# An attention stage with folded projections, and a latent loop regrouped by heads and written out

## What is computed

```python
h = h + attn(layernorm(h))                # 8 heads of width 128, biases on q, k and v, softmax, @ Wo
h = h + latent(layernorm(h))

# latent: G=8 groups of H=16 heads, D=128, L=100 latents
xn = l2norm(x) * gamma
q = xn @ Wq + bq ; k, v = split(xn @ Wkv + bkv)
w = (softmax(silu(k @ aw1 + b) @ aw2 + b, -1) / s + softmax(.., -2) / L) / 2
kc, vc = einsum('bsd,bsl->bld', k, w), einsum('bsd,bsl->bld', v, w)   # per group
att = softmax(q . kc / sqrt(D))           # b, g, h, s, l
z = att . vc                              # 16384 wide per token
h1 = silu(l2norm(z) * g1 @ W1 + b1)       # 256 wide
out = silu(l2norm(h1) * g2 @ W2 + b2)
```

## Time and profile before

| | us |
|---|---|
| median of 3 runs | 3341.05 |
| the runs | 3330.03 to 3342.83 |
| the profiled execution | 3334.86 |
| its span, first to last instruction | 3332.0 |
| attention, 704.9 to 1315.4 | 610.5 |
| latent prologue, 1318.4 to 1383.3 | 64.9 |
| latent loops with both tails, 1383.3 to 3332.0 | 1948.7 |

### The profile page before, as it was taken

How to read it: one execution, slowest core, us unless ns; L and a number is a source line. 1 busy time by engine, 2 the same in 40 slices (tenths; PEclk the granted TensorE clock), 3 DMA queues, 4 the chain that set the end, 5 groups by cost and what they waited for, 6 DMA issues and landing times.

```text
span 3332.0 us, 57433 instructions
## 1 busy us (share of the span) xinstructions
PE 3032.7 (91%) x18996; PEld 2666.2 (80%) x19032; DVE 2402.0 (72%) x4368; ACT 1797.5 (54%) x3135; POOL 1772.1 (53%) x1524
## 2 busy tenths in 40 slices
PE   3488885979999998799999999999799999999997
PEld 3266664868888887599999999998699999999986
DVE  2499896356676676577777777776677777777774
ACT  0398893446566564255555555554455555555544
POOL 5698883010100001366666666675467666666663
PEclk9899996989999999799999999999899999999998
DMA  1111100000000001000000000000000000000000
GB/s 43 40 29 24 25 20 26 0 35 0 0 0 0 0 0 46 19 30 29 28 28 28 28 28 19 28 28 29 10 29 28 28 28 28 28 28 28 28 27 7
DMA packets 36972, 75.92 MB, mean 23 GB/s; under 512 B 9644, under 2 KB 13876, under 8 KB 36120
## 3 DMA queue, kind: packets, MB, share of 16 engines
q1 hardware_dynamic: 35352, 71.68, 6.8%
q0 software_dynamic: 1536, 3.15, 0.4%
HBM read 65.36 MB, written 1.05 MB: 20 GB/s over the span
## 4 chain that ended last, share of the span: by engine, by line
PE 49%; issue 5%; POOL 3%; DVE 1%; ACT 0%; POOLq 0%; DVEq 0%; ACTq 0%
PE lat_ps_h L1837 20%; PE lat_ps_z L1851 10%; PE lat_ps_s L1763 7%; PE lat_ps_t L1790 6%; PE lat_ps_z L1781 3%; POOL lat_zz L1570 2%; PE lat_ps_z L1773 2%; PE lat_ps_z L1861 1%; POOL latm_wq L1549 0%; POOL latm_wq L1543 0%; POOL latm_att L1562 0%; POOL latm_vcg L1554 0%; PE lat_ps_s L1879 0%; DVE latm_norm L1669 0%; DVE latm_h L1675 0%
## 5 line engine op out<-in xcount | busy, mean ns | idle before, releaser
L1837 PE MATMUL lat_ps_h<-latm_share,latm_attT 100*128 100x256 f32 x6144 | 885.9, 286 | 0.0
L1837 PEld LDWEIGHTS lat_ps_h<-latm_share,latm_attT 100*128 100x128 f32 x6144 | 818.7, 189 | 24.0 <-DVE latm_attT L1626 11.1
L1562 POOL TENSOR_TENSOR latm_att<-latm_sc,latm_tot 128x400 f32<-128x400 f32 x516 | 440.6, 854 | 618.7 <-DVE latm_tot L1621 592.2
L1570 POOL TENSOR_TENSOR lat_zz<-lat_zz,lat_zsq 128x512 f32<-128x512 f32 x514 | 659.7, 1283 | 0.3
L1698 ACT ACTIVATE latm_sc<-latm_sc 128x400 f32<-128x400 f32 x516 | 278.4, 539 | 430.8 <-DVE latm_sc L1612 430.8
L1851 PE MATMUL lat_ps_z<-latm_attT,latm_vg 100*128 100x512 f32 x1536 | 486.8, 425 | 0.0
L1619 DVE TENSOR_REDUCE latm_tot<-latm_sc 128x4 f32<-128x400 f32 x516 | 290.9, 564 | 156.9 <-ACT latm_sc L1698 156.9
L1626 DVE TENSOR_TENSOR latm_attT<-lat_ps_t,latm_attT 100x512 fp32r<-100x512 f32 x514 | 349.8, 681 | 61.3 <-ACT latm_attT L1714 61.3
L1714 ACT CAST latm_attT<-lat_ps_t 100x512 fp32r<-100x512 f32 x514 | 300.3, 584 | 147.8 <-PE lat_ps_t L1790 122.8
L1763 PE MATMUL lat_ps_s<-latm_wk,lat_xr 128*128 128x400 f32 x1548 | 370.1, 348 | 3.0 <-issue 3.0
L1719 ACT ACTIVATE lat_zsq<-lat_ps_z 128x512 f32<-128x512 f32 x512 | 306.9, 599 | 59.1 <-PE lat_ps_z L1851 22.2
(11 more groups left out here) (339 smaller groups left out, 4816.0 us busy)
## 6 DMA issues: line engine op xcount, KB each, us to landing
lat_w_in<-in_w_quads SPq DMA_DIRECT2D x65, 512.0 KB, 3.6
lat_wq_in<-in_wq_quads SPq DMA_DIRECT2D x65, 256.0 KB, 2.6
ret_qk_head<-ret_qk_parts SPq DMA_DIRECT2D x256, 32.0 KB, 2.0
moe_w<-in_W SPq DMA_DIRECT2D x2, 1024.0 KB
mha_wqk<-in_Wqk SPq DMA_DIRECT2D x1, 1152.0 KB, 5.4
ret_shared<-in_xpos_q SPq DMA_DIRECT2D x1, 1024.0 KB, 5.6
ret_shared<-in_xpos_k SPq DMA_DIRECT2D x1, 1024.0 KB, 4.9
latw_wkv<-in_Wkv SPq DMA_DIRECT2D x1, 1024.0 KB
```

The source lines that it names most:

```text
L1562: nc.gpsimd.tensor_tensor(att[:, u].rearrange("p (j l) -> p j l", j=QH), sc[:, u].rearrange("p (j l) -> p j l", j=QH), tot[:, u].unsqueeze ...
L1570: nc.gpsimd.tensor_tensor(zz[:, t], zz[:, t], zsq[:, u], ALU.add).then_inc(s["zz_added"], 1)
L1837: mm = e.matmul(ps_h[:, t, :], attT[:, t % 2, a_part, j * P:(j + 1) * P], share[:, u, w_part, j * FF2:(j + 1) * FF2], start=False, stop=Fa ...
```

## The change

Attention. Wq and Wk of each head are multiplied once into one matrix, Wv and Wo likewise, with the biases (`fold`, `fold_bias`; the means of Wq and Wk are first taken out on VectorE and added on GpSimd). q is no longer made: scores are xr (the normed input plus one, `lift`) times keys made with the folded matrix. v with Wo in it lands directly in the output's space, so that `output` goes, and all heads of a sequence add up in PSUM. That needs probabilities that are divided before they are turned: GpSimd multiplies the 128x1024 tile by the inverse sum. The 128 steps are written out, with scores two steps ahead and `gather` seven behind.

Latent loop. The step is now one head with four tiles: `add` uses share as stationary operand and attT (512 tokens) as moving one, 6 products of 512 columns in place of 12 of 256; the result is kept transposed (`ps_h` is [feature, token]), so that the tail needs no transposes. Scores, with their softmax, run LEAD = 6 steps ahead of the addition, with 8 slots of `att`. wk and share go into the free bank of ps_s, after the scores. All 512 steps (both sequences) are written out as one row; the tail of the first sequence is put into steps of the second (`MIDDLE`), that of the second starts in its last steps (`ENDING`). Square roots and silu are made from Newton steps on VectorE and tanh on ScalarE.

```diff
+        @block.gpsimd                       # attention
+            e.wait_ge(weights_in, 112)
+            nc.gpsimd.tensor_copy(bv_wide[:], bv[:].unsqueeze(2).to_broadcast([P, H, P])).then_inc(s["bv_widened"], 1)
+            e.wait_ge(s["qk_mean"], START + 2)
+            nc.gpsimd.tensor_tensor(wqT[:], wqT[:], wide(mean[:, 0]), ALU.add).then_inc(s["q_centred"], 1)
+            nc.gpsimd.tensor_tensor(wkT[:], wkT[:], wide(mean[:, 1]), ALU.add).then_inc(s["k_centred"], 1)
...
+            for step in range(K):
+                e.wait_ge(s["inv_ready"], START + step + 1)
+                nc.gpsimd.tensor_scalar(probs[:, step % 4], probs[:, step % 4], inv[:, step % TB:step % TB + 1], None, ALU.mult
+                                        ).then_inc(s["normed"], 1)
+                if step >= 1 and makes_values(step - 1):
+                    low_values(*makes_values(step - 1))
...
+            fold()                          # attention, tensor
             norm.tensor(e)
+            fold_bias()
...
+            for step in range(K + 14):
+                if LAG <= step < K + LAG:
+                    gather(step)
+                if step >= 1 and makes_keys(step - 1):
+                    n, c = makes_keys(step - 1)
+                    e.wait_ge(s["keys_ready"], START + 2 * n + c + 1)
...
+                if 2 <= step <= K + 1:
+                    turn(step - 2)
+                if step + 2 < K:
+                    score(step + 2)
+                if makes_keys(step):
+                    make_keys(n, c, psT[:, 0, :])
+                if makes_values(step):
+                    make_values(n, half, psT[:, 0, :])
...
+            norm.vector(e, means)           # attention, vector: means stands ahead of sum_squares
...
+                def add(n):                 # latent, tensor
...
+                    for a_part, w_parts in ((0, (0, 1)), (1, (0,))):
+                        if a_part == 1:
+                            e.wait_ge(s["attT_ready"], START + n + 1)
+                        for f in range(2):
+                            for w_part in w_parts:
+                                cols = slice(j * FF2 + f * P, j * FF2 + (f + 1) * P)
+                                mm = e.matmul(ps_h[:, f, half, :], share[:, q % 2, w_part, cols], attT[:, n % 2, a_part],
...
-                for a_part, w_part in ((0, 0), (0, 1), (1, 0)):
-                    for j in range(QH):
-                        mm = e.matmul(ps_h[:, t, :], attT[:, t % 2, a_part, j * P:(j + 1) * P],
-                                      share[:, u, w_part, j * FF2:(j + 1) * FF2],
...
+                def turn(n):
+                    half, j = n % TB // 4, n % 4
+                    if j == 0:
+                        e.wait_ge(s["weighted"], START + n + 4)
+                    e.wait_ge(s["attT_ready"], START + n)
+                    for i in range(4):
+                        mm = e.transpose(ps_t[0:L, i * P:(i + 1) * P], att[:, (n - j + i) % SLOTS, j * L:(j + 1) * L], ident[:])
...
+                for n in range(-LEAD, END):
+                    k = n + LEAD
+                    if n - 1 >= -LEAD:
+                        free_spare(n - 1)
+                    if k < K:
+                        score(k)
+                    if makes_wk(n):
+                        e.wait_ge(s["shifted"], START + k)
+                        make_wk(quad(k) + 1, spare_bank(n))
+                    if makes_share(n):
+                        e.wait_ge(s["shifted"], START + k)
+                        make_share(quad(n) + 1, n % TB - 4, spare_bank(n))
...
+                    if 0 <= n < K:
+                        add(n)
+                    if 0 <= n + 1 < K:
+                        turn(n + 1)
+                    if 0 <= n < K:
+                        reduce_heads(n)
...
+                def inverse_root(which, step, floor, done):   # latent, vector
+                    x, y = sums[:, which], inv[:, which]
...
+                        c.then(e.tensor_tensor(newton[:], y, y, ALU.mult))
+                        c.then(e.tensor_tensor(newton[:], newton[:], x, ALU.mult))
+                        c.then(e.tensor_scalar(newton[:], newton[:], -0.5, 1.5, ALU.mult, ALU.add))
+                        c.then(e.tensor_tensor(y, y, newton[:], ALU.mult))
...
+            MIDDLE = {"norm": 0, "root": 0, "spread": 4, "wide": 8, "scale": 8, "tanh": 9, "gate": 10, "square": 10,
+                      "power": 16, "power_root": 16, "result": 24, "pre": 24, "out_tanh": 24, "out": 25}
```

More of the change, by code:

```diff
@@ L1008, in _ @@
[L1008 to L1018 removed]
+            wide = lambda a: a.unsqueeze(2).to_broadcast([P, H, D])
+            e.wait_ge(weights_in, 112)
@@ L1059, in _ @@
[L1059 to L1087 removed]
+            e.wait_ge(s["wqk_ready"], START + 1)
@@ L1131, in _ @@
+            for step in range(K + 14):
+                if step < K:
+                    exponentials(step)
+                for b, c in closes(step):
+                    keep_out(b, c)
+                if 2 <= step <= K + 1:
+                    high(step - 2)
+                if step >= 1 and makes_values(step - 1):
+                    high_values(*makes_values(step - 1))
+                if makes_keys(step):
+                    high_keys(*makes_keys(step), psT[:, 0, :])
         @block.vector
@@ new lines, in low, with add_out @@
+            def low(k):
+                i = k % TB
+                for half in range(2):
+                    high, rest = (probsT[:, part, 4 * half:4 * half + 4, i * P:(i + 1) * P] for part in range(2))
+                    e.wait_ge(s[f"high_ready{half}"], START + k + 1)
+                    e.tensor_tensor(rest, psT[:, half, :].rearrange("p (j s) -> p j s", j=4), high.bitcast(F32),
+                                    ALU.subtract).then_inc(s[f"low_ready{half}"], 1)
+            def add_out(b, c):
+                t = b * TB + 4 * c
+                e.wait_ge(s["out_turned"], START + 2 * b + c + 1)
+                e.tensor_tensor(h[:, t:t + 4], psT[:, 0, :].rearrange("p (t d) -> p t d", t=4), h[:, t:t + 4], ALU.add).then_inc(s["out_added"], 1)
@@ new lines, in _ @@
+            for c in range(2):
+                low_keys(0, c, psS[:, 0, c, :])
+            e.wait_ge(s["bvo_ready"], START + 1)
+            for half in range(2):
+                full_values(0, half, psO[:, half, :])
+            maxima(0)
+            for step in range(K + 14):
+                if step + 1 < K:
+                    maxima(step + 1)
+                if 2 <= step <= K + 1:
+                    low(step - 2)
+                if step < K:
+                    invert(step)
+                if makes_keys(step):
+                    low_keys(*makes_keys(step), psT[:, 0, :])
+                if makes_values(step):
+                    full_values(*makes_values(step), psT[:, 0, :])
+                for b, c in adds_out(step):
+                    add_out(b, c)
@@ new lines, in latent, with when, due, rooting @@
+            STEPS = 4
+            END = K + 8
+            def when(b, c, stage):
+                if b == 0:
+                    return NS + TB + 4 * TB * c + MIDDLE[stage]
+                return ENDING[c][stage]
+            def due(n, stage):
+                return [(i, b, c) for i, (b, c) in enumerate(units) if when(b, c, stage) == n]
+            def rooting(n, stage):
+                done = []
+                for i, (b, c) in enumerate(units):
+                    per = 1 if b == 0 else 2 if (c, stage) == (0, "root") else STEPS
+                    first = per * (n - when(b, c, stage))
+                    done += [(i, step) for step in range(first, first + per) if 0 <= first < STEPS]
+                return done
@@ new lines, in root_of_power, with scale_h @@
+                def root_of_power(i, step):
+                    if step == 0:
+                        e.wait_ge(s["power_kept"], START + i + 1)
+                        e.wait_ge(s["pre_ready"], START + i)
+                    inverse_root(1, step, 4e-24 / FF2, "power_inverted")
+                def scale_h(i, half, bank):
+                    e.wait_ge(s["wide_ready"], START + i + 1)
+                    e.wait_ge(s["h_kept"], START + 2 * i + 2)
+                    for f in range(2):
+                        c.then(e.tensor_tensor(hT[:, half, f], bank, hT[:, half, f], ALU.mult))
+                    e.sem_inc(s["h_scaled"], 1)
+                    for f in range(2):
+                        last = e.tensor_scalar(hT[:, half, f], hT[:, half, f], b1[:, f:f + 1], None, ALU.add)
+                    last.then_inc(s["h_biased"], 1)
```

1173 lines of the change are left out of this document (593 added, 580 removed).

## The result

The changed kernel takes 3195.83 us in the median (3195.40 to 3197.89) against 3335.54 for the kernel before: a ratio of 0.958, with an interval of 0.956 to 0.961. Forecast were 3248 and a range of 3170 to 3310. The gain is 140 us where 93 were expected. The profiled execution has a span of 3194.1 us.

A forecast was written before the change was run, and what follows sets the result against it. TensorE was taken as the bound, 99% busy in both loops and 97% in the attention. Gains of 38 + 34 + 11 - 3 + 13 = 93 us gave 3248 us by the median; range to give 3170 to 3310.

The forecast's parts named there:

- rival A: Latent loop: TensorE's edges and gaps go, steps 3.02, a quad 27.3 or so; 70 us more gained, 3178; chance 0.20.
- Attention, steady part: Attention units: 33.3 us each in place of 36.28, as q's and the output's products go; gain 49 us.
- rival B: Attention: GpSimd's tensor_scalar takes 4.1, units come to about 36, the gain of 49 shrinks to 6; 3291; chance 0.13.
- Attention, start: Before the first attention unit: means wait for all weight transfers, folding runs on slow TensorE; 11 us later, bounds 4 and 17.
- Latent step: Plain latent steps: time goes by columns, so regrouping to 512 columns gives 0; steps stay 3.10, bounds +31 and -41 us.
- The quad: Four latent steps with wk and two shares inserted: extra falls from 3.67 to 3.47; latent steps gain 34, bounds 100 and -40.
- t = 2: Latent step ahead of wk, VectorE's late step of 3.37: 0.27 goes, as the mean of wq moves behind the low part.
- First tail: First sequence's tail, moved into the second loop: 48.4 us go, 37 come in, 1.3 a root step; gain 11, bounds 19 and 65.
- End: Second sequence's tail at the kernel's end: 44.3 us become about 31; gain 13, bounds 22 and 4.
- C: Latent loop: VectorE blocked at every root and inserted steps at their upper bound; 3320; chance 0.08.
- D: Latent loop: `turn` with j == 0 waits for weighted probabilities, forecast ready 0.9 us early; if late, 256 us more, 3504; chance 0.05.
- E: Attention: the folding removes no TensorE work, so the change doesn't do what it says; given nothing.

The follow-up runs named there:

- pool_longer: Changed kernel with an additional GpSimd product of 128x416 ahead of each attention weighting; 3280.2 us on another chip, 57 us more from the attention on.
- before_bank: Kernel before, with wk and the two shares put into the free bank of the scores (ps_s) in place of ps_z; 3304.6 us.
- before_bank_mean: before_bank with the mean of wq moved on VectorE from behind the shift to behind the low part of the additions; 3354.9 us.
- before_unrolled: Kernel before with only its latent loop written out, eight copies in place of the hardware loop; 3324.3 us.
- before_bank_unrolled: before_bank with its latent loop written out; 3314.5 us on another chip, 19 us less than before_bank from the attention on.

## Why the prediction was right, and where it was wrong

The direction was forecast, and the attention with its mechanism; the size of the whole was not: 93 us of gain were forecast and 140 came. 3195.8 lies outside the forecast's own 3215 to 3285, and it is inside the range given because that was widened for rival A, whose mechanism did not come: that part is luck. One term was badly off, the inserted work of a quad.

- Attention, steady part: right to the tenth, in part because two terms were off in opposite ways. Timeline of TensorE, first half of v for the second and the sixteenth unit; and the group of GpSimd's product:

```profile
766.87 1.05 PE L986 MATMUL mha_psT<-mha_wvo,xT 128*128 128x128 f32 x8
...
1232.35 1.05 PE L986 MATMUL mha_psT<-mha_wvo,xT 128*128 128x128 f32 x8
```
```profile
L946 POOL TENSOR_SCALAR mha_probs<-mha_probs,mha_inv x128: 2841/2848/2858, 747.4 to 1266.7; 128x1024 f32<-128x1024 f32 x128
```

  (1232.35 - 766.87) / 14 = 33.25, forecast 33.3. By distances from scores to scores, eight plain steps are 3.65 each (forecast 3.71, 0.5 less a unit), the keys with their wait 2.2 (forecast 1.9), the values 1.8 (1.7). GpSimd's product takes 2.85, forecast 3.0: rival B's 4.1 was the wrong row, but its mechanism and its price of 36 a unit hold, as pool_longer shows (4.24 a step, 36.47 a unit).
- Attention, start: first scores 35.5 us after the first transfer against 23.8 before, 11.7 later; forecast 11, by the same chain (means behind all transfers, GpSimd's additions, folding on a slow TensorE).
- Latent step: 1.40 for the additions, right; six products fewer are worth 0.09 a quad. Plain steps of 3.08, not 3.10: 0.16 a quad.
- The quad: the term that was mis-sized. The forecast took one quad of the earlier trace rows, whose three steps are 3.67 longer than plain ones (3.49 in the mean of 27), called that work but for 0.4, of which it took half as gone, and left 3.47. After the change 2.67 is left (0.95 + 0.86 + 0.86), and the rest had been waiting. A quad went from 28.60 to 27.31: 0.65 for the bank ps_z, shown by before_bank; 0.23 in the step of wk (4.26 to 4.03), which before_bank didn't remove; 0.27 of t = 2, foreseen; 0.15 in plain steps and shares, 0.09 of it the regrouping. The miss is 0.96 a quad, 60 us; the 0.80 of it in the inserted work lies just inside the bound of 0.9 less.
- The 0.23 is for the most part a wait for GpSimd, which centres wq before wk is made from it. Timeline of GpSimd and TensorE, before_bank first (wk, then a share for comparison), then the changed kernel:

```profile
1722.07 1.03 POOL L1549 TENSOR_TENSOR latm_wq<-latm_wq,latm_wq_sum 128x512 f32<-128x512 f32 x1
1722.28 0.71 PE L1763 MATMUL lat_ps_s<-latm_wk,lat_xr 128*128 128x400 f32 x3
1722.83 0.40 PE L1839 MATMUL lat_ps_h<-latm_share,latm_attT 100*128 100x256 f32 x2
1723.26 1.13 PE L1773 MATMUL lat_ps_s<-lat_kcT,latm_wq 128*128 x8
...
1727.12 0.40 PE L1839 MATMUL lat_ps_h<-latm_share,latm_attT 100*128 100x256 f32 x2
1727.36 1.03 PE L1781 MATMUL lat_ps_s<-lat_w_in,latm_vcg 128*100 128x256 f32 x4
```
```profile
1700.36 1.04 POOL L1626 TENSOR_TENSOR latm_wq<-latm_wq,latm_wq_sum 128x512 f32<-128x512 f32 x1
```

  In before_bank wk begins 0.43 us after two products that hold a share back for only 0.24, and L1549 ends at 1723.10, 0.82 into the step. In the changed kernel L1626 ends at 1701.40, 0.39 into the step that begins at 1701.01, while the scores still run, and wk follows them at 1701.55 without a wait. In the means of 28 quads wk begins 0.29 after the start of the last product ahead of it, against 0.12 for a share, so TensorE waits 0.17 there, and not at all in the changed kernel. In before_bank_mean, where the centring ends 1.4 us ahead of wk, the 0.29 are 0.12 as well. No run moved the centring alone.
- The row itself misled. The earlier trace rows put 0.22 ahead of wk on "issue", and the forecast took it for the cost of loop registers. Written out, the idle time of the weight loads there stays, 12.8 us in all in before_unrolled, put down to ScalarE's square, and 12.2 in before_bank_unrolled, where that square is no longer waited for, on "issue"; in the kernel before the profile names GpSimd's centring in 33 cases and "issue" in 32. So most of it wasn't the registers, which are worth 0.12 in that step, and the name alone decides nothing.
- t = 2: right in its size, wrong in its reason. The move alone makes the kernel slower (before_bank_mean); it is free in the changed kernel, by the order on ScalarE as far as the timelines tell.
- First tail: 39.7 against 37, with blocked VectorE operations as described. The earlier trace rows had shown it: 161 ns free, 736 in the median. The Trainium skill (SBUF — State Buffer, Who interferes with whom) has this rule for two SBUF inputs and for `tensor_scalar`, which can take both ports; both agree, L1737 with 1.22 against 0.16 and L1738 with 0.79 against 0.17. The forecast's 1.3 a root step lay between free and all blocked, as the steps did.
- Fill: 5.9 later, forecast 3. End: 34.25, forecast 31; two powers and two results of 16 small instructions each take 14 us there (3171.2 to 3185.6), at a granted clock of 0.50, the lower of its two levels (0.63 over the whole end).
- Rivals. A's time, 3178, is nearer than the forecast's, and its quad of 27.3 came, but not from edges: steps are 3.08, not 3.02. The prediction's sentence under A that L1763 shows no stall across quads overlooked the one at 3170.60. C's blocking came, its price for inserted work didn't. D stayed away: in the first sequence the tile that `turn` needs is weighted 1.4 to 1.7 us ahead, not the 0.9 estimated. In one case L1641 ends at 1702.21 and L1977 begins at 1703.91. Beside the roots of the first tail only 0.26 is left at the least. E is out with the attention's 37 us.

## What to carry to other kernels

When extra work sits in a pipelined loop, compare its cost with its own instructions' time before calling it work: here 3.49 us held 2.67 of products, and the rest was a PSUM bank shared with the product z and a wait for an input that GpSimd finished late. Put such work into a bank whose last reader is long done, and let what it needs be ready before its place in the step comes. Small VectorE operations belong where GpSimd waits, and one move on one engine is to be read against the fixed order of the next: a mean moved alone made a quad 0.6 us longer where 0.27 less was expected. And look at every row of a kind: a stall at one of seven branches doesn't show in an average.

## What the runs showed of the hardware

- An operation of four numbers a partition on VectorE takes 0.16 us (L1737), or until GpSimd's running instruction ends, up to 1.22, also with a single input (L1738, 0.17 or up to 1.22).
- A hardware loop can lose 1.5 to 3.0 us at a branch, on issue: at seven of seven in one program, at one of seven in another of nearly the same size; written out, at none.
- GpSimd's product with a column of scalars: 2.85 us for 1024 columns, 1.32 for 416.
